# A graph network whose last three tiles, padding alone, are no longer gathered or scattered row by row

## Chip, cores and metric

The kernel runs on one core of a Trainium2 chip. The metric is the device time of one execution in microseconds (us); the median of three runs of the kernel before is 15976.06 us (15976.02, 15976.06 and 15996.48).

## What is computed

12500 nodes with 64 features and 212500 edges, sorted by destination, go through four graph layers. Each of them reads a row of a node table for every edge, computes a message from it and sums the messages by node. Cut to what matters here:

```python
# L0: softmax over the nodes gives attn; then
msg = h[src][:, None, :] * attn[src][:, :, None]
neigh = segment_sum(msg, dst, n)
# L1: two linear halves of [x[row], x[col]], relu, sum by row
# L2: three GAT layers
e = leaky_relu(alpha_src[src] + alpha_dst[dst], 0.2)
m = segment_max(e, dst, n)
ex = exp(e - m[dst])
out = segment_sum(alpha[:, :, None] * h[src], dst, n)
# L3: a three-layer network on [x[src], edge_attr], then sum by dst, then on the nodes
```

The output is the 12500 x 64 node table after L3.

## The kernel before

The edges are padded to 212992 = 1664 tiles of 128 edges. Sixteen tiles are a group (`GT = 16`), four groups a turn of the loops (`G4`, with four sets of buffers), and there are `TURNS = 26` turns. A padding edge has node 12500 at both ends, one row past the real ones. The real edges fill 1660 tiles and 20 rows of tile 1660, so tile 1660 holds 108 padding edges, and tiles 1661 to 1663, the last three of group k = 3 of the last turn, hold nothing else.

The program is a row of phases. A phase (`Phase.run`, line 91) gives each engine its own instruction stream, and ends with a barrier of all engines (lines 93 to 105). There the profile shows a DRAIN of each engine. Six phases run over all 1664 tiles with one indirect DMA per tile on GpSimd (POOL):

- `first_pass` (phase e0): gathers 64 floats per edge; TensorE multiplies them with the 0/1 matrix of equal destinations (`sums`, line 560) and counts edges per node (`counts`); GpSimd at 406 to 416, TensorE's loop at 579 to 585.
- `sort_rows` (phase sort1): computes for each edge a destination in the order of the other end, and scatters its row of 65 floats to `sorted_rows` (GpSimd at 1027 to 1041); the next phase (`carried_pass`) reads them.
- `gat_pass` three times (phases eg1, eg2, eg3): gathers 136, 136 and 65 floats per edge; VectorE starts a group when its 16 gathers have landed (line 1388, then the operation of line 1390).
- `attr_pass` (phase e3): gathers 128 floats per edge; TensorE starts a group's first quad of tiles when the 16 gathers have landed (`pe_first`, line 1622, operations of lines 1594 and 1595).

GpSimd's program is the same in the five gathering phases: a loop of 26 turns, in it the four groups, in each a wait for the row numbers (`loaded`), a wait per four tiles for the buffers (`summed`) and 16 calls of `gather` (line 112). Each gather adds 16 to the semaphore `gathered[k]`; the reader waits for all 16 gathers of a group at once. In the sorting phase the calls are of `scatter` (line 117), and GpSimd waits at the end for all that moved (line 1041). TensorE, VectorE and ScalarE have their last turn written out already in sort1, eg1 to eg3 and (TensorE and ScalarE) e3; GpSimd has all 26 turns in the loop everywhere, and TensorE has in e0. After a gathering phase, `finish_sums` reads what the phase stored.

Of the kernel before, what the change touches and what calls it, by code (L numbers as in the profile page):

```python
# [38 lines left out]
G4 = range(4)  # L39
B2 = range(2)  # L40
TURNS = NG // len(G4)
assert T % P == 0 and QT * DE == P and NT % CHUNK == 0 and N < P * P


# [83 lines left out]
def row_numbers(e, ve, c, out, pos, tmp):  # L128

    e.tensor_scalar(out, pos, 0x7FFFFFFF ^ (GROUP - 1), None, ALU.bitwise_and).then_inc(ve, 1)  # L130
    e.tensor_scalar(tmp, pos, P - 1, 4, ALU.bitwise_and, ALU.logical_shift_left).then_inc(ve, 1)
    e.wait_ge(ve, c(2))
    e.tensor_tensor(out, out, tmp, ALU.bitwise_or).then_inc(ve, 1)
    e.wait_ge(ve, c(1))
    e.tensor_scalar(tmp, pos, 7, GT - 1, ALU.logical_shift_right, ALU.bitwise_and).then_inc(ve, 1)
    e.wait_ge(ve, c(1))
    e.tensor_tensor(out, out, tmp, ALU.bitwise_or).then_inc(ve, 1)
    e.wait_ge(ve, c(1))


def broadcast_row(row, n):
# [27 lines left out]
class Kernel:  # L169
# [126 lines left out]
    def first_pass(self, table, out, last):  # L296
# [109 lines left out]
        def gpsimd(e):  # L406
            for k in G4:
                e.dma_start(ph.prime(), self.ident[0:16, 0:1]).then_inc(gathered[k].sem, 16)
            with e.Fori(0, TURNS) as it:
                for k in G4:  # L410
                    e.wait_ge(loaded[k].sem, loaded[k].at(it, 1))
                    for t in range(GT):
                        if t % QT == 0:
                            e.wait_ge(summed.sem, summed.at(it, (k + 1) * QUADS - U + t // QT))
                            e.sem_inc(turns, 1)
                        gather(e, got[k][:, t, :], table[:, :], rows[k][:, t, 1:2]).then_inc(gathered[k].sem, 16)

        def vector(e):
            e.sem_inc(equaled.sem, equaled.ahead)
# [124 lines left out]
        def tensor(e):  # L544
            e.sem_inc(summed.sem, summed.ahead)
            e.sem_inc(counted.sem, counted.ahead)
            e.wait_ge(set_up, 1)
            e.matmul(ps_count[:, :, :], zero[:, 0:P], zero[:, :], start=True, stop=False)

            def spread_keys(it, q):  # L550
                k, tiles = at(q)
                if q % QUADS == 0:
                    e.wait_ge(keyed.sem, keyed.at(it, k + 1))
                e.wait_ge(equaled.sem, equaled.at(it, q - 1))
                for i in range(QT):
                    t = tiles.start + i
                    last_i = e.transpose(ps_key[q % 2][:, i, :], key[k][:, t:t + 1].to_broadcast([P, P]), self.ident[:, :])  # L557
                last_i.then_inc(spread.sem, 1)

            def sums(it, q):  # L560
                k, tiles = at(q)
                e.wait_ge(gathered[k].sem, gathered[k].at(it, 1))
                e.wait_ge(equaled.sem, equaled.at(it, q + 1))
                e.wait_ge(copied.sem, copied.at(it, q - 1))
                for i in range(QT):
                    t = tiles.start + i
                    last_i = e.matmul(ps_sum[q % 2][:, i, 0:D], equal[k % 2][:, t, :], got[k][:, t, :], start=True, stop=True)  # L567
                last_i.then_inc(summed.sem, 1)

            def counts(it, q):  # L570
                e.wait_ge(hots.sem, hots.at(it, q + 1))
                e.wait_ge(hots_a.sem, hots_a.at(it, q + 1))
                for i in range(QT):
                    for end in B2:
                        last_i = e.matmul(ps_count[:, end, :], hot[q % 2][:, 0, end, i, :], hot[q % 2][:, 1, end, i, :],
                                          start=False, stop=False)
                last_i.then_inc(counted.sem, 1)

            with e.Fori(0, TURNS) as it:
                for q in range(U + 1):  # L580
                    if q < U:
                        spread_keys(it, q)
                    if q:
                        counts(it, q - 1)
                        sums(it, q - 1)
            e.matmul(ps_count[:, :, :], zero[:, 0:P], zero[:, :], start=False, stop=True).then_inc(opened, 1)
            e.wait_ge(scanned, 2)
            e.matmul(off_ps[:, :], self.above[:, :], incl[:, :, P - 1], start=True, stop=True).then_inc(offsets, 1)
# [197 lines left out]
    def sort_rows(self):  # L786
# [47 lines left out]
        numbers = Tally(ph, "numbers", 5 * n4)  # L834
        placed = Tally(ph, "placed", n4)
        moved = [Tally(ph, f"moved{k}", 1, GT * 16, ahead=16) for k in G4]
        first, table0, ready, turns = (ph.sem(k) for k in ("first", "table0", "ready", "turns"))

        def at(q):
            k, i = divmod(q, QUADS)  # L840
# [186 lines left out]
        def gpsimd(e):  # L1027
            for k in G4:
                e.dma_start(ph.prime(), self.ident[0:16, 0:1]).then_inc(moved[k].sem, 16)
            with e.Fori(0, TURNS) as it:  # L1030
                for k in G4:
                    e.wait_ge(placed.sem, placed.at(it, k + 1))
                    e.wait_ge(carried.sem, carried.at(it, (k + 1) * 2))
                    e.sem_inc(turns, 1)
                    for t in range(GT):
                        if t and t % QT == 0:
                            e.wait_ge(look_read.sem, look_read.at(it, (k + 1) * QUADS + t // QT - 2))
                            e.sem_inc(turns, 1)
                        scatter(e, self.sorted_rows, dest[k][:, t:t + 1], rows[k][:, t, :]).then_inc(moved[k].sem, 16)
            for k in G4:  # L1040
                e.wait_ge(moved[k].sem, moved[k].at(0, TURNS))
        ph.run(sync=sync, vector=vector, tensor=tensor, scalar=scalar, gpsimd=gpsimd)

    def carried_pass(self, values, out, last):
# [169 lines left out]
    def gat_pass(self, name, table, out, last, values, heads, ch):  # L1214
# [82 lines left out]
        def gpsimd(e):  # L1297
            for k in G4:
                e.dma_start(ph.prime(), self.ident[0:16, 0:1]).then_inc(gathered[k].sem, 16)
            with e.Fori(0, TURNS) as it:  # L1300
                for k in G4:
                    e.wait_ge(loaded[k].sem, loaded[k].at(it, 1))
                    for t in range(GT):
                        if t % QT == 0:
                            e.wait_ge(summed.sem, summed.at(it, (k + 1) * QUADS - U + t // QT))
                            e.sem_inc(turns, 1)
                        gather(e, got[k][:, t, :], table[:, :], rows[k][:, t, 1:2]).then_inc(gathered[k].sem, 16)

        def dve_key(e, it, k):
            e.wait_ge(loaded[buf(k)].sem, loaded[buf(k)].at(it, 1 + k // len(G4)))  # L1310
# [56 lines left out]
        def dve_stage(e, it, new, mid, old):  # L1367
# [17 lines left out]
                e.tensor_copy(c3[:, 2], r[:, 1]).then_inc(cuts.sem, 1)  # L1385
            if mid is not None:
                e.wait_ge(filled.sem, filled.at(it, mid + 1))
                e.wait_ge(gathered[buf(mid)].sem, gathered[buf(mid)].at(it, 1 + mid // n4))
                e.wait_ge(message.sem, message.at(it, mid))
                e.tensor_tensor(diff[:, :, :], by_tile(sm[:, 1, 0:W]), rows_mid[:, :, HF:FG], ALU.add).then_inc(scores.sem, 1)  # L1390
                e.wait_ge(scores.sem, scores.at(it, 4 * mid + 1))
                e.scalar_tensor_tensor(score[:, :, :], diff[:, :, :], 0.2, diff[:, :, :], ALU.mult, ALU.max).then_inc(scores.sem, 1)  # L1392
# [88 lines left out]
    def attr_pass(self, name, table, out, last, weights, own_weights):  # L1481
# [59 lines left out]
        def gpsimd(e):  # L1541
            for k in G4:
                e.dma_start(ph.prime(), self.ident[0:16, 0:1]).then_inc(gathered[k].sem, 16)
            with e.Fori(0, TURNS) as it:
                for k in G4:
                    e.wait_ge(loaded[k].sem, loaded[k].at(it, 1))
                    for t in range(GT):
                        if t % QT == 0:
                            e.wait_ge(summed.sem, summed.at(it, (k + 1) * QUADS - U + t // QT))
                            e.sem_inc(turns, 1)  # L1550
                        gather(e, got[k][:, t, :], table[:, :], rows[k][:, t, 1:2]).then_inc(gathered[k].sem, 16)

        def pe_own_turn(e, b):
            ts = own_quads[b]
# [32 lines left out]

        def pe_first(e, it, q):
            k, tiles = at(q)
            e.wait_ge(gathered[k % n4].sem, gathered[k % n4].at(it, 1 + k // n4))  # L1590
            e.wait_ge(attr_down.sem, attr_down.at(it, q + 1))
            e.wait_ge(relued.sem, relued.at(it, q - 1))
            for i in range(QT):
                e.transpose(ps_first[q % 2][:, i, :], got[k % n4][:, tiles.start + i, :], self.ident[:, :])  # L1594
                last_i = e.matmul(ps_first[q % 2][:, i, :], w_attr[:, i, :], attr_t[q % 4][:, :], start=False, stop=True,  # L1595
                                  skip_group_check=True)
            last_i.then_inc(first.sem, 1)
# [1481 lines left out]
```

## Time and profile before

| | |
|---|---|
| median of three runs | 15976.06 us |
| the profiled execution | 15981.7 us |
| its span, first to last instruction | 15980.0 us |
| granted TensorE clock, mean | 0.697 |
| POOL busy | 11257.5 us, 70% |
| PE (matmul) busy | 8190.7 us, 51% |
| VectorE (DVE) busy | 6692.7 us, 42% |
| ScalarE (ACT) busy | 5666.0 us, 35% |
| indirect DMAs of the six phases | 4992 + 3328 gathers, 1664 scatters |
| software DMA queue (GpSimd's) | 361120 packets, 582.27 MB, 15.9% of the 16 engines |

All rows are of one execution. A busy time of POOL in an indirect DMA is the time in which it makes the descriptors, not the time in which the data moves. A time after "idle before" is how long the engine had nothing to do before the instruction, and "<-" says what ended that. A wait that ended with a landing is read as: the instruction started when the DMA's data had arrived.

### The profile page before, as it was taken

How to read it: one execution, taken by the hardware profiler on the slowest of the kernel's cores; microseconds unless marked ns; L12 is line 12 of the kernel's file. 1: busy time of each engine (PE TensorE's matmuls, PEld its weight loads, DVE VectorE, ACT ScalarE, POOL GpSimd, SP SyncE). 2: the span in 40 equal slices, each digit the busy share in tenths (PEclk: the TensorE clock that was granted, in tenths of full speed). 3: DMA queues.
4: the chain of work that ended last, by engine and by line, in shares of the span. 5: the costliest groups of instructions: out<-in, count | busy, mean ns of one | idle time of the engine just before them, and what ended most of it. 6: DMA issues, size and time to landing. Idle time of an engine off the chain costs nothing. (4 is left out here: it accounts for less than half of the span.)

```text
span 15980.0 us, 259817 instructions
## 1 busy us (share of the span) xinstructions
PE 8190.7 (51%) x75456; PEld 7411.3 (46%) x75456; DVE 6692.7 (42%) x24144; ACT 5666.0 (35%) x13371; POOL 11257.5 (70%) x11862
## 2 busy tenths in 40 slices
PE   6555552565664763434432444432344444888886
PEld 4555441455554653333332333332344443777775
DVE  5555554777775863333335333335222224211112
ACT  2555551677774531222221222221111112333332
POOL 4777767677775457777767777776777775577776
PEclk9776765878877975666665666665555555799998
DMA  4444442222223743444432444443333332344443
GB/s 153 162 161 162 162 142 57 96 93 91 92 93 120 257 155 93 146 146 146 146 117 72 146 146 146 146 143 60 77 85 85 85 85 54 119 146 146 146 146 97
DMA packets 895395, 1965.03 MB, mean 123 GB/s; under 512 B 392230, under 2 KB 471026, under 8 KB 854067
## 3 DMA queue, kind: packets, MB, share of 16 engines
q0 software_dynamic: 361120, 582.27, 15.9%
q1 hardware_dynamic: 426179, 797.11, 14.6%
q10 hardware_dynamic: 107776, 582.40, 9.5%
q14 instruction: 243, 1.99, 0.0%
q8 instruction: 77, 1.26, 0.0%
HBM read 1095.74 MB, written 894.54 MB: 125 GB/s over the span
## 5 line engine op out<-in xcount | busy, mean ns | idle before, releaser
L112 POOL DMA_INDIRECT eg_got<-gat_table,eg_rows x4992 | 4714.7, 944 | 1542.1 <-issue 1512.5
L112 POOL DMA_INDIRECT e_got<-table,e_rows x3328 | 3155.6, 948 | 1031.2 <-issue 1004.6
L1321 PE MATMUL eg_ps_sum<-eg_got,eg_equal 128*128 128x136 f32 (+1 forms) x9984 | 2070.8, 382 | 280.3 <-DVE eg_got L1409 256.5
L1328 ACT ACTIVATE eg_outs<-eg_ps_sum 128x544 f32<-128x544 f32 (+1 forms) x1248 | 675.1, 541 | 4279.2 <-PE eg_ps_sum L1321 4268.9
L1321 PEld LDWEIGHTS eg_ps_sum<-eg_got,eg_equal 128*128 128x128 f32 x9984 | 1965.5, 291 | 344.2 <-ACT eg_outs L1328 189.1
L117 POOL DMA_INDIRECT sorted_rows<-sort_rows,sort_dest x1664 | 1615.9, 971 | 532.8 <-issue 495.9
L1353 PE MATMUL eg_small<-ident,eg_score 128*128 128x128 f32 (+1 forms) x312 | 138.6, 444 | 3176.1 <-DVE eg_score L1392 3176.1
L1353 PEld LDWEIGHTS eg_small<-ident,eg_score 128*128 128x128 f32 (+1 forms) x312 | 47.2, 151 | 3203.5 <-DVE eg_score L1392 3203.5
L1390 DVE TENSOR_TENSOR eg_diff<-eg_small,eg_got 128x128 f32<-128x128 f32 (+1 forms) x312 | 79.1, 253 | 2732.6 <-DMA eg_got<-gat_table,eg_rows 2732.6
L1621 DVE TENSOR_SCALAR e_got<-e_ps_second 128x512 f32<-128x512 f32 x416 | 287.6, 691 | 1758.0 <-PE e_ps_second L1604 1727.5
L567 PE MATMUL e_ps_sum<-e_got,e_equal 128*128 128x64 f32 x3328 | 628.8, 352 | 676.1 <-DMA e_got<-table,e_rows 676.1
L1421 ACT ACTIVATE eg_equal<-eg_equal_b 128x512 f32<-128x512 bf16 x1248 | 778.4, 624 | 469.1 <-issue 271.5
L567 PEld LDWEIGHTS e_ps_sum<-e_got,e_equal 128*128 128x128 f32 x3328 | 586.7, 265 | 694.6 <-DMA e_got<-table,e_rows 374.8
L449 DVE TENSOR_SCALAR e_hot<-iota_free,e_part_f 128x128 bf16<-128x128 bf16 x4992 | 880.2, 277 | 0.0
L897 DVE SCALAR_TENSOR_TENSOR sort_junk<-sort_ps_bc,sort_num,sort_before 128x128 bf16<-128x128 f32 (+3 forms) x1664 | 814.7, 545 | 48.2 <-PE sort_ps_bc L946 47.2
L496 ACT ACTIVATE e_dist<-iota_free,e_part_f 128x128 bf16<-128x128 bf16 x1664 | 528.2, 389 | 558.2 <-DVE e_part_f L437 378.9
L443 DVE TENSOR_TENSOR e_equal<-e_ps_key,e_key 128x512 f32<-128x512 f32 x416 | 286.4, 688 | 936.2 <-PE e_ps_key L557 932.9
L1594 PE MATMUL e_ps_first<-ident,e_got 128*128 128x128 f32 x1664 | 489.3, 294 | 368.0 <-DMA e_got<-table,e_rows 368.0
L1595 PE MATMUL e_ps_first<-e_attr_t,w_w_attr 128*128 128x128 f32 x3328 | 634.8, 293 | 0.0
L1206 POOL TENSOR_TENSOR e_cut<-e_rest,e_cut 128x256 bf16<-128x256 f32 x416 | 301.5, 725 | 460.8 <-ACT e_cut L1182 460.8
L1409 DVE TENSOR_TENSOR eg_got<-eg_got,eg_small 128x2048 f32<-128x2048 f32 (+1 forms) x312 | 602.7, 1932 | 10.6
L1595 PEld LDWEIGHTS e_ps_first<-e_attr_t,w_w_attr 128*128 128x128 f32 x3328 | 558.6, 210 | 0.0
(528 smaller groups left out, 20828.1 us busy)
## 6 DMA issues: line engine op xcount, KB each, us to landing
gat_out<-eg_outs ACTq DMA_DIRECT2D x208, 1152.0 KB
eg_equal_b<-equal_d SPq DMA_DIRECT2D x312, 512.0 KB
out<-e_outs ACTq DMA_DIRECT2D x208, 512.0 KB
out<-e_outs ACTq DMA_DIRECT2D x104, 1024.0 KB
values<-e_zeros_b SPq DMA_DIRECT2D x104, 768.0 KB
values_q<-e_zeros_b SPq DMA_DIRECT2D x104, 768.0 KB
sort_value<-values_q SPq DMA_DIRECT2D x104, 768.0 KB
e_value<-values SPq DMA_DIRECT2D x104, 768.0 KB
```

Of the source, the lines that this page charges most:

```text
L112: return e.indirect_dma_start(out, None, table, bass.IndirectOffsetOnAxis(ap=index, axis=0), **kw)
L117: return e.indirect_dma_start(table, bass.IndirectOffsetOnAxis(ap=index, axis=0), rows, None, **kw)
L449: last_i = e.tensor_scalar(hot[q % 2][:, a, end, i, :], self.iota_free[:, :], part_f[k % 2][:, a, end, t:t + 1], None, ALU.is_equal)
L496: e.activation(dist[q % 2][:, i, :], self.iota_free[:, :], ACT.Abs, scale=-1.0, bias=part_f[k % 2][:, 1, 1, t:t + 1]).then_inc(dist_made.s ...
L567: last_i = e.matmul(ps_sum[q % 2][:, i, 0:D], equal[k % 2][:, t, :], got[k][:, t, :], start=True, stop=True)
L897: last = e.scalar_tensor_tensor(junk[n - 1][:, 0:n, :], ps_bc[q % 2][:, 0:n, :], num[k % n4][:, 2, t:t + 1], before[:, QT - n:QT, :], ALU. ...
L1321: last_i = e.matmul(ps_sum[q % 2][:, i, 0:FG], equal[q % 4][:, i, :], got[k][:, t, :], start=True, stop=True)
L1328: e.activation(outs[k % 2][:, tiles, 0:FG], ps_sum[q % 2][:, :, 0:FG], ACT.Copy).then_inc(copied.sem, 1)
L1409: e.tensor_tensor(hs, hs, over(weight, ch), ALU.mult).then_inc(message.sem, 1)
L1421: e.activation(equal[q % 4][:, :, :], equal_b[buf(k)][:, tiles, :], ACT.Copy).then_inc(equaled.sem, 1)
L1594: e.transpose(ps_first[q % 2][:, i, :], got[k % n4][:, tiles.start + i, :], self.ident[:, :])
L1595: last_i = e.matmul(ps_first[q % 2][:, i, :], w_attr[:, i, :], attr_t[q % 4][:, :], start=False, stop=True, skip_group_check=True)
```

## The change

`REAL` counts the real tiles of each group of the last turn: [16, 16, 16, 13]. GpSimd's loop takes 25 turns, and the last one is written out with `REAL[k]` tiles. The readers of the last group wait for 13 gathers instead of 16 (`arrived`). In the sorting phase, the last three tiles, which stay where they are in the sorted order, are copied by one direct DMA of 128 partitions x 780 bytes, with a semaphore of its own. TensorE's loop in `first_pass` gets its last turn written out too, so that the wait can differ there. The arithmetic on the three tiles stays; it reads what an earlier group left in the buffer, and its results go to the padding node alone.

```diff
+REAL = [min(GT, max(0, -(-E // P) - ((TURNS - 1) * len(G4) + k) * GT)) for k in G4]
...
+def arrived(gathered, it, k):
+    buf, turn = k % len(G4), k // len(G4)
+    missing = GT - REAL[buf] if isinstance(it, int) and it + turn == TURNS - 1 else 0
+    return gathered[buf].at(it, 1 + turn) - 16 * missing
...
 # first_pass, gat_pass and attr_pass, GpSimd
-            with e.Fori(0, TURNS) as it:
+            def group(it, k, tiles):
+                e.wait_ge(loaded[k].sem, loaded[k].at(it, 1))
+                for t in range(tiles):
+                    if t % QT == 0:
+                        e.wait_ge(summed.sem, summed.at(it, (k + 1) * QUADS - U + t // QT))
+                        e.sem_inc(turns, 1)
+                    gather(e, got[k][:, t, :], table[:, :], rows[k][:, t, 1:2]).then_inc(gathered[k].sem, 16)
+            with e.Fori(0, TURNS - 1) as it:
                 for k in G4:
...
+                    group(it, k, GT)
+            for k in G4:
+                group(TURNS - 1, k, REAL[k])
 # first_pass, TensorE
-                e.wait_ge(gathered[k].sem, gathered[k].at(it, 1))
+                e.wait_ge(gathered[k].sem, arrived(gathered, it, k))
...
-            with e.Fori(0, TURNS) as it:
+            def turn(it):
                 for q in range(U + 1):
...
+            with e.Fori(0, TURNS - 1) as it:
+                turn(it)
+            turn(TURNS - 1)
 # sort_rows, GpSimd: group() as above with scatter; after the tiles of a group
+                if tiles < GT:
+                    e.dma_start(by_group(self.sorted_rows)[it * n4 + k, :, tiles:, :], rows[k][:, tiles:, :]).then_inc(tail_moved, 16)
...
+            for k in G4:
+                e.wait_ge(moved[k].sem, moved[k].at(0, TURNS) - 16 * (GT - REAL[k]))
+            e.wait_ge(tail_moved, 16 * sum(tiles < GT for tiles in REAL))
 # gat_pass, VectorE, and attr_pass, TensorE: the same arrived() in the wait for the gathers
```

## Rows read from the trace of the kernel before

**Rows 1.** Groups by line, engine POOL: count | busy us, mean ns | idle before.
```profile
L112 POOL DMA_INDIRECT eg_got<-gat_table,eg_rows x4992 | 4714.7, 944 | 1542.1 <-issue 1512.5 <-DMA eg_rows<-pairs_d 21.3 <-PE eg_ps_sum L1321 8.2
L117 POOL DMA_INDIRECT sorted_rows<-sort_rows,sort_dest x1664 | 1615.9, 971 | 532.8 <-issue 495.9 <-ACT sort_rows L1015 26.3 <-DVE sort_base L907 10.7
L112 POOL DMA_INDIRECT g1c_agg<-gat_out,end_row x98 | 125.5, 1281 | 36.9 <-issue 29.3 <-DVE g1c_agg L2822 7.6
```

**Rows 2.** Timeline of e0's end: start us, us busy, what [idle before].
```profile
2342.01 0.94 POOL L112 DMA_INDIRECT e_got<-table,e_rows  x1 [0.30 <-issue]
2344.55 1.97 PE L567 MATMUL e_ps_sum<-e_got,e_equal 128*128 128x64 f32 x8 [6.70 <-DMA e_got<-table,e_rows]
...
2362.07 0.94 POOL L112 DMA_INDIRECT e_got<-table,e_rows  x1 [0.30 <-issue]
2367.68 1.97 PE L567 MATMUL e_ps_sum<-e_got,e_equal 128*128 128x64 f32 x8 [9.60 <-DMA e_got<-table,e_rows]
```

**Rows 3.** Timelines, ends of eg1 and eg2.
```profile
8228.99 0.94 POOL L112 DMA_INDIRECT eg_got<-gat_table,eg_rows  x1 [0.30 <-issue]
8231.58 0.29 DVE L1390 TENSOR_TENSOR eg_diff<-eg_small,eg_got 128x128 f32<-128x128 f32 x1 [8.45 <-DMA eg_got<-gat_table,eg_rows]
8248.98 0.94 POOL L112 DMA_INDIRECT eg_got<-gat_table,eg_rows  x1 [0.30 <-issue]
8253.74 0.29 DVE L1390 TENSOR_TENSOR eg_diff<-eg_small,eg_got 128x128 f32<-128x128 f32 x1 [13.59 <-DMA eg_got<-gat_table,eg_rows]
...
10780.84 0.94 POOL L112 DMA_INDIRECT eg_got<-gat_table,eg_rows  x1 [0.30 <-issue]
10785.35 0.29 DVE L1390 TENSOR_TENSOR eg_diff<-eg_small,eg_got 128x128 f32<-128x128 f32 x1 [12.85 <-DMA eg_got<-gat_table,eg_rows]
```

**Rows 4.** DMA queues: GpSimd's queue in 2347:2357 and in 2363:2368: packets, MB, share.
```profile
q0 software_dynamic: 256, 0.26, 14.1%
...
q0 software_dynamic: 67, 0.07, 31.9%
```

**Rows 5.** Timeline of e3's end.
```profile
15753.65 0.94 POOL L112 DMA_INDIRECT e_got<-table,e_rows  x1 [0.30 <-issue]
15754.05 0.27 PE L1586 MATMUL e_ps_at<-ident,e_attrs 128*128 128x128 f32 x1
15758.79 0.48 PE L1594 MATMUL e_ps_first<-ident,e_got 128*128 128x128 f32 x1 [4.46 <-DMA e_got<-table,e_rows]
```

**Rows 6.** Windows of e3's end: length, busy (x count) by engine, PEclk, DMA share, GB/s.
```profile
15742.84:15754.30 11.46, 11.46 (x93) 10.20 (x91) 2.07 (x3) 5.69 (x13) 8.72 (x10) 1.00 0.28 51
15758.79:15763.90 5.11, 5.11 (x31) 4.66 (x32) 0.69 (x1) 1.12 (x2) 0.00 (x0) 0.73 0.36 149
```

**Rows 7.** Timeline of sort1's end.
```profile
5020.47 0.97 POOL L117 DMA_INDIRECT sorted_rows<-sort_rows,sort_dest  x1 [0.30 <-issue]
...
5023.01 0.96 POOL L117 DMA_INDIRECT sorted_rows<-sort_rows,sort_dest  x1 [0.30 <-issue]
5032.99 0.35 SPq L1103 DMA_DIRECT2D e_group_f<-sorted_rows  x1
```

**Rows 8.** POOL's sequencer at sort1's end, line 93: durations ns, first and last start.
```profile
L93 POOLq DRAIN  x1: 6603/6603/6603, 5025.5 to 5025.5; - x1
```

**Rows 9.** The first direct DMAs of GpSimd in eg3, and SP's wait for the first.
```profile
11217.50 2.06 POOL L1299 DMA_DIRECT2D eg_prime<-ident  x4 [4.41 <-POOLq L105]
11223.92 0.35 SPq L1293 DMA_DIRECT2D eg_rows<-pairs_d  x1
```

**Rows 10.** POOL's sequencer, the branch of e0's loop (line 409), all turns.
```profile
L409 POOLq COMPARE_BRANCH  x26: 40/45/53, 342.3 to 2348.0; - x26
```

**Rows 11.** Timeline: written-out gathers beside a VectorE scan.
```profile
2406.86 3.62 DVE L1837 TENSOR_TENSOR_SCAN f_run<-links,f_acc_t 64x1664 f32<-64x1664 bf16 x1 [7.43 <-ACT f_acc_t L1813]
2407.49 3.74 POOL L112 DMA_INDIRECT f_pr_spans<-span,first_key  x1 [0.30 <-issue]
2411.53 0.94 POOL L112 DMA_INDIRECT f_pr_spans<-span,first_key  x1 [0.30 <-issue]
```

More of the change, by code:

```diff
@@ L408, in gpsimd @@
                 e.dma_start(ph.prime(), self.ident[0:16, 0:1]).then_inc(gathered[k].sem, 16)
-            with e.Fori(0, TURNS) as it:
-                for k in G4:
[L411 to L416, printed above, removed]
+            def group(it, k, tiles):
[6 more added lines that the diff above has]
+            with e.Fori(0, TURNS - 1) as it:
+                for k in G4:
+                    group(it, k, GT)
+            for k in G4:
+                group(TURNS - 1, k, REAL[k])
         def vector(e):
@@ L836, in sort_rows @@
         moved = [Tally(ph, f"moved{k}", 1, GT * 16, ahead=16) for k in G4]
-        first, table0, ready, turns = (ph.sem(k) for k in ("first", "table0", "ready", "turns"))
+        first, table0, ready, turns, tail_moved = (ph.sem(k) for k in ("first", "table0", "ready", "turns", "tail_moved"))
         def at(q):
@@ L1029, in gpsimd, with group @@
                 e.dma_start(ph.prime(), self.ident[0:16, 0:1]).then_inc(moved[k].sem, 16)
-            with e.Fori(0, TURNS) as it:
-                for k in G4:
[L1032 to L1039, printed above, removed]
+            def group(it, k, tiles):
+                e.wait_ge(placed.sem, placed.at(it, k + 1))
+                e.wait_ge(carried.sem, carried.at(it, (k + 1) * 2))
+                e.sem_inc(turns, 1)
+                for t in range(tiles):
+                    if t and t % QT == 0:
+                        e.wait_ge(look_read.sem, look_read.at(it, (k + 1) * QUADS + t // QT - 2))
+                        e.sem_inc(turns, 1)
+                    scatter(e, self.sorted_rows, dest[k][:, t:t + 1], rows[k][:, t, :]).then_inc(moved[k].sem, 16)
+                if tiles < GT:
+                    e.dma_start(by_group(self.sorted_rows)[it * n4 + k, :, tiles:, :], rows[k][:, tiles:, :]).then_inc(tail_moved, 16)
+            with e.Fori(0, TURNS - 1) as it:
+                for k in G4:
+                    group(it, k, GT)
             for k in G4:
-                e.wait_ge(moved[k].sem, moved[k].at(0, TURNS))
+                group(TURNS - 1, k, REAL[k])
+            for k in G4:
+                e.wait_ge(moved[k].sem, moved[k].at(0, TURNS) - 16 * (GT - REAL[k]))
+            e.wait_ge(tail_moved, 16 * sum(tiles < GT for tiles in REAL))
         ph.run(sync=sync, vector=vector, tensor=tensor, scalar=scalar, gpsimd=gpsimd)
@@ L1299, in gpsimd, with group @@
                 e.dma_start(ph.prime(), self.ident[0:16, 0:1]).then_inc(gathered[k].sem, 16)
-            with e.Fori(0, TURNS) as it:
-                for k in G4:
[L1302 to L1307, printed above, removed]
+            def group(it, k, tiles):
+                e.wait_ge(loaded[k].sem, loaded[k].at(it, 1))
+                for t in range(tiles):
+                    if t % QT == 0:
+                        e.wait_ge(summed.sem, summed.at(it, (k + 1) * QUADS - U + t // QT))
+                        e.sem_inc(turns, 1)
+                    gather(e, got[k][:, t, :], table[:, :], rows[k][:, t, 1:2]).then_inc(gathered[k].sem, 16)
+            with e.Fori(0, TURNS - 1) as it:
+                for k in G4:
+                    group(it, k, GT)
+            for k in G4:
+                group(TURNS - 1, k, REAL[k])
         def dve_key(e, it, k):
@@ L1387, in dve_stage @@
                 e.wait_ge(filled.sem, filled.at(it, mid + 1))
-                e.wait_ge(gathered[buf(mid)].sem, gathered[buf(mid)].at(it, 1 + mid // n4))
+                e.wait_ge(gathered[buf(mid)].sem, arrived(gathered, it, mid))
                 e.wait_ge(message.sem, message.at(it, mid))
@@ L1543, in gpsimd, with group @@
                 e.dma_start(ph.prime(), self.ident[0:16, 0:1]).then_inc(gathered[k].sem, 16)
-            with e.Fori(0, TURNS) as it:
-                for k in G4:
[L1546 to L1551, printed above, removed]
+            def group(it, k, tiles):
+                e.wait_ge(loaded[k].sem, loaded[k].at(it, 1))
+                for t in range(tiles):
+                    if t % QT == 0:
+                        e.wait_ge(summed.sem, summed.at(it, (k + 1) * QUADS - U + t // QT))
+                        e.sem_inc(turns, 1)
+                    gather(e, got[k][:, t, :], table[:, :], rows[k][:, t, 1:2]).then_inc(gathered[k].sem, 16)
+            with e.Fori(0, TURNS - 1) as it:
+                for k in G4:
+                    group(it, k, GT)
+            for k in G4:
+                group(TURNS - 1, k, REAL[k])
         def pe_own_turn(e, b):
@@ L1589, in pe_first @@
             k, tiles = at(q)
-            e.wait_ge(gathered[k % n4].sem, gathered[k % n4].at(it, 1 + k // n4))
+            e.wait_ge(gathered[k % n4].sem, arrived(gathered, it, k))
             e.wait_ge(attr_down.sem, attr_down.at(it, q + 1))
```

## The prediction

> **What bounds the kernel now.** I read the groups by line first. In the six phases that run over all 1664 tiles, POOL makes an indirect DMA's descriptors for 944 to 971 ns, then sits for some 300 ns, and nearly all of that idle time is "issue": it waits for nobody [rows 1]. From the eg row, (4714.7 + 1542.1) / 4992 = 1.253 us per gather on average; at the ends of the phases a step is 0.94 + 0.30 = 1.25 us [rows 2, 3]. From the sort row (1615.9 + 532.8) / 1664 = 1.29 us, at its end 1.27 [rows 7]. So the phases go at POOL's pace, and what matters is what their last group hangs on.
>
> Next I read the timelines of the ends. In e0, TensorE has been idle 9.60 us when the last group's gathers have landed [rows 2]. In eg1 and eg2 VectorE has been idle about 13 us, and eg3 is built the same way [rows 3]. In e3 TensorE has been idle 4.46 us [rows 5]. In the sorting phase the last scatter starts at 5023.01; once GpSimd's wait for the landings is over, its DRAIN of 6.6 us begins, at 5025.5, and the next phase starts at 5032.99 [rows 7, 8]. In all six ends the last indirect DMA is on the path, and everything behind it is a chain that moves with it.
>
> A second thing is to be seen there. A group's data are ready 1.60 us after its last gather was issued in an ordinary group (2342.95 to 2344.55), but 4.67 us after it in the last group (2363.01 to 2367.68) [rows 2]. In eg1 it is 1.65 against 3.82 us [rows 3]. Packets on GpSimd's queue explain it: 14.1% of 16 engines x 10 us over 256 packets is 88 ns each in ordinary tiles, and 31.9% of 16 x 5 us over 67 is 381 ns each at e0's end [rows 4]. The last four tiles are those whose edges (108, 128, 128 and 128 of 128) all read the same row of the table. I call the 4.67 - 1.60 us, and its like in the other phases, the excess.
>
> **The change, part by part.**
> *Issue time.* In each of e0, eg1, eg2 and eg3 three gathers go: 3 x 1.25 = 3.75 us, four times is 15.0 us. All of it is on the path, since the engine that waits has been idle for longer.
> *The excess.* e0: 4.67 - 1.60 = 3.07. eg1: 3.82 - 1.65 = 2.17. eg2: 10781.78 to 10785.35 is 3.57, less 1.65: 1.92 [rows 3]. eg3 repeats the pattern, and I count it like eg2. Sum 9.1. Tile 1660 with its 108 equal rows stays last, so not all of it goes. Bounds: nothing of it goes, or all. The excess builds up over four nearly equal gathers and three of them go, so I take three quarters: 6.8 us.
> *e3.* Here the idle time caps the gain. TensorE is done with the group before at 15754.3 (its last matmul, 15754.05 + 0.27), and the landing moves from 15758.79 to about 15754.59 - 3.75 + 2.5 = 15753.3, so TensorE's 4.46 us idle time vanishes, and no more [rows 5]. But after that idle time the clock stood at a mean of 0.73 in the first quad, which took 5.1 us (15758.79 to 15763.90); without a stall three quads take 11.46 us, 3.8 each, at a clock of 1.00 [rows 6]. That is up to 1.3 us more, of which I take 1.0, since the clock need not be up from the first matmul on. Sum 5.5 us; from below 3.75 (the landing's tail stays as long, no clock), from above 6.
> *The sorting phase.* Three scatters go; the direct copy takes the place of the first (5020.47). It waits for nothing of its own and has 13 scatters ahead of it in GpSimd's queue. The trace has no copy of this shape. From a scatter's start to the DRAIN, with its landing between them, it is 2.5 us (5023.01 to 5025.5) [rows 7, 8]. The direct DMAs at the start of eg3 take 2.06 / 4 = 0.5 us each of GpSimd, and SP, which waits for the first, goes on 6.4 us after its start (11217.50 to 11223.92) [rows 9]. So the DRAIN would begin between 5021.0, if the copy landed with its own issue, and 5026.9: a gain of 4.5 to a loss of 1.4. I take the scatter's time, being the nearest in partitions and place: 5023.0, a gain of 2.5 us. The DRAIN behind it I leave at 6.6 us; that its length changes by a microsecond with what lies in the queue can't be excluded. The added wait on `tail_moved` has nothing behind it but that DRAIN.
> *The written-out turns.* GpSimd's sequencer took the loop's last branch at 2348.0, while the last gather began at 2362.07 [rows 2, 10]: it runs 14 us, some eleven gathers, ahead of the engine. Leaving the loop one turn earlier and reading code that is used once is hidden behind these. TensorE's written-out turn in e0 is hidden behind its waits for gathers (6.70 us before group k = 2 of the last turn, with its 16 ordinary gathers) [rows 2]; without that cover each microsecond of it counts. I cost both at nothing. What is late next, once the stalls are shorter, is TensorE itself in e3; in e0 and eg1 to eg3 it is still the landing.
>
> Sum: 15.0 + 6.8 + 5.5 + 2.5 = 29.8 us. Against the profiled execution that is 15981.7 - 29.8 = 15951.9; the median of the runs lies 5.6 us lower, which gives 15946 us.
>
> **The rivals.**
> *Only the issue time goes* (nothing of the excess). Tile 1660 is nearly all padding, and if one such gather is enough to keep the packets slow, the landing's tail stays. For it: the packets that land last are the slowest. Against it: gathers overlap, and at 88 ns per packet before them the slowness is theirs alone [rows 4]. Gain 15.0 + 3.75 + 2.5 = 21.3: 15955 us. A page would have it so: the Trainium skill, "DMA: Bandwidth & Descriptors", section on the anatomy of one DMA on the GpSimd path, gives each such DMA a fixed 2.0 us plus its bytes over the bandwidth, whatever rows it reads; a gather of eg1 (69632 bytes) would be there 2.2 us after its start, in the last tile as in any. The trace disagrees: 8248.98 to 8253.74 is 4.76 us [rows 3].
> *All of the excess goes*, with e3 at its best: 15.0 + 9.1 + 6 + 2.5 = 32.6: 15943.5 us.
> *Written-out gathers are slow: slower than before.* Place: the written-out turn on GpSimd, 61 DMAs in six phases. The straight-line gathers of g1c cost (125.5 + 36.9) / 98 = 1.66 us each, 0.40 more than in the loops [rows 1]. At that price 6 x 61 x 0.40 = 148 us are added, 118 net: 16094 us. It turns the sign from 0.08 us per gather on. Against it: another straight line of gathers takes 0.94 us each, as the loops do, except one of 3.74 us that lies over a VectorE scan of 3.62 [rows 11]. So the slowness comes from what VectorE does beside them, not from the code. The Trainium skill, "SBUF — State Buffer", section on the two sides of SBUF, says that a VectorE operation that holds the port pair shared with GpSimd keeps it from writing descriptors; by that rule, and by the trace, straight code costs nothing of itself.
> *The change does nothing that can be measured*: something else, such as the stores, ends the phases. The idle times of rows 2 and 3 speak against it. 15976 us.
>
> **How the numbers follow.** A difference of 0.2%, 32 us, is about what a measurement of this kernel tells from none; 15944 is that bound. Chances: my forecast (26 to 31 us less) 0.56, all of the excess 0.22, only the issue time 0.15, slower 0.03, nothing 0.04. Single runs of one kernel lie up to 20 us apart, so I give each case some 6 us to both sides: of the forecast 0.21 falls beyond the bound, of the second case 0.16, of the third 0.01. Together faster 0.38, the same 0.58, slower 0.04. Range: the largest gain, 15.0 + 9.1 + 6 + 4.5 = 35, gives 15941, with the measurement 15936. The smallest sum of the bounds, 15.0 + 0 + 3.75 - 1.4 - 1 = 16, gives 15960, with the measurement 15966.
>
> **What would show it.** Right: 4983 and 3322 gathers at an unchanged 0.94 us; in e0 to eg3 the wait's end 5.2 to 6.0 us earlier counted from the phase's first gather, 2.0 to 2.4 us behind the last gather's end; in e3 no idle TensorE before its last group, and a clock of 1.00 there; a copy that lands 2 to 3 us after its start and a DRAIN of about 6.6 us. Wrong: idle time above 0.30 us between GpSimd's DMAs in the last turn, TensorE short of code in e0's last turn, a copy that holds the wait past 5025, or a tail behind the last gather that stays at 3.6 us and more.

## The result and the profile after

The changed kernel's median is 15951.62 us (15945.77 to 15954.14, 22 runs), that of the kernel before on the same chip 15979.92 us (15976.02 to 15996.48, 22 runs). The ratio is 0.9982, with a 95% interval of 0.9975 to 0.9988: 28.3 us less by the medians. The profiled executions say 15953.09 against 15981.7 us, 28.6 us less. Forecast were 15946 us and a gain of 29.8.

The groups of POOL after the change, by line (they answer to [rows 1]); columns as there:

```profile
L113 POOL DMA_INDIRECT eg_got<-gat_table,eg_rows x4983 | 4705.4, 944 | 1538.8 <-issue 1511.5 <-DMA eg_rows<-pairs_d 20.8 <-PE eg_ps_sum L1350 6.4
L113 POOL DMA_INDIRECT e_got<-table,e_rows x3322 | 3149.4, 948 | 1030.9 <-issue 1002.2 <-DMA e_rows<-pairs_d 16.0 <-PE e_ps_sum L1649 11.8
L118 POOL DMA_INDIRECT sorted_rows<-sort_rows,sort_dest x1661 | 1612.7, 971 | 532.0 <-issue 492.2 <-ACT sort_rows L1031 26.1 <-DVE sort_base L923 13.4
```

Three operations fewer per phase, each as long as before, and the idle time is still "issue". Now the ends, after the change, as a timeline; first e0 (against [rows 2]):

```profile
2342.20 0.95 POOL L113 DMA_INDIRECT e_got<-table,e_rows  x1 [0.30 <-issue]
...
2357.31 0.95 POOL L113 DMA_INDIRECT e_got<-table,e_rows  x1 [0.30 <-issue]
2360.65 1.97 PE L580 MATMUL e_ps_sum<-e_got,e_equal 128*128 128x64 f32 x8 [4.13 <-DMA e_got<-table,e_rows]
```

The last group has 13 gathers, and its data are ready 2.39 us behind the last one's end (2358.26 to 2360.65); before it was 4.67. TensorE still waits for them, 4.13 us instead of 9.60. In eg1, eg2 and eg3 (against [rows 3]) VectorE starts 2.4 to 2.5 us behind the last gather's end:

```profile
8237.92 0.29 DVE L1419 TENSOR_TENSOR eg_diff<-eg_small,eg_got 128x128 f32<-128x128 f32 x1 [6.78 <-DMA eg_got<-gat_table,eg_rows]
...
10765.20 0.29 DVE L1419 TENSOR_TENSOR eg_diff<-eg_small,eg_got 128x128 f32<-128x128 f32 x1 [7.41 <-DMA eg_got<-gat_table,eg_rows]
...
13285.47 0.18 DVE L1419 TENSOR_TENSOR eg_diff<-eg_small,eg_got 128x16 f32<-128x16 f32 x1 [7.99 <-DMA eg_got<-gat_table,eg_rows]
```

In e3 (against [rows 5]) the wait before the last group is gone. The first row below is the last matmul of group k = 2, the second and third are the last group's, without idle time before them:

```profile
15731.21 1.06 PE L1649 MATMUL e_ps_sum<-e_got,e_equal 128*128 128x128 f32 x8
15732.10 0.27 PE L1620 MATMUL e_ps_at<-ident,e_attrs 128*128 128x128 f32 x1
15732.21 0.27 PE L1628 MATMUL e_ps_first<-ident,e_got 128*128 128x128 f32 x1
```

And the windows of the same stretch (against [rows 6]): the last group's first 11.46 us are done at the full clock, as the group before it.

```profile
15720.64:15732.10 11.46, 11.46 (x94) 10.42 (x93) 2.32 (x4) 5.64 (x12) 5.78 (x7) 1.00 0.18 42
...
15732.10:15743.56 11.46, 11.46 (x95) 10.42 (x94) 2.08 (x3) 5.62 (x12) 0.00 (x0) 1.00 0.23 94
```

The sorting phase's end, timeline and POOL's sequencer (against [rows 7, 8]):

```profile
5012.69 0.96 POOL L118 DMA_INDIRECT sorted_rows<-sort_rows,sort_dest  x1 [0.30 <-issue]
5013.65 0.61 POOL L1056 DMA_DIRECT2D sorted_rows<-sort_rows  x1
5023.22 0.35 SPq L1127 DMA_DIRECT2D e_group_f<-sorted_rows  x1
```

```profile
L94 POOLq DRAIN  x1: 6440/6440/6440, 5015.9 to 5015.9; - x1
```

**Where the time went.** Whole phases are poor measures here: earlier stalls make one and the same phase up to 2 us longer or shorter between executions (e0 of the changed kernel took 2115.4 us in one execution and 2117.3 in another). What is comparable is the end of a phase: from the start of the last group's first gather or scatter to the clearing of the phase's semaphores (in e0 after the change 2342.20 to 2392.16). I use it for all kernels:

| us | e0 | sort1 | eg1 | eg2 | eg3 | e3 | sum |
|---|---|---|---|---|---|---|---|
| before | 55.47 | 28.52 | 41.97 | 42.32 | 40.88 | 52.19 | 261.35 |
| after | 49.96 | 25.26 | 37.55 | 36.89 | 36.01 | 46.90 | 232.57 |
| less | 5.51 | 3.26 | 4.42 | 5.43 | 4.87 | 5.29 | 28.78 |
| forecast | 6.0 | 2.5 | 5.4 | 5.2 | 5.2 | 5.5 | 29.8 |

The forecast row is the prediction's, its 6.8 us of excess shared out by its own shares. The six ends hold the whole gain of 28.6 us. Between them single stretches differ, but the differences cancel: from the clearing behind eg2 to eg3's first gather it is 425.9 us after the change and 422.1 before, and the other stretches are together as much shorter.

### The profile page after: what moved, and what is told of

The parts are those of the page before. It is cut to its first block and busy times, and to the rows that moved or that the text cites. A ratio compares the mean times of both kernels' runs of the same rounds, so it can differ in the third digit from the quotient of the medians.

```text
span 15951.4 us, 259671 instructions
## 1 busy us (share of the span) xinstructions
PE 8184.6 (51%) x75456; PEld 7411.5 (46%) x75456; DVE 6693.9 (42%) x24144; ACT 5665.9 (36%) x13371; POOL 11240.2 (70%) x11845
## 5 line engine op out<-in xcount | busy, mean ns | idle before, releaser
L970 PE MATMUL sort_ps_table<-sort_hot_lo,sort_hot_hi 128*128 128x128 bf16 x1664 | 187.9, 244 | 728.0 <-ACT sort_table L1022 727.2
```

## The experiments

Each was timed beside the kernel before on the same chip. Single executions of one kernel differ by 5 to 20 us, so a difference of 3 or 4 us is read from the ends of the phases, and the medians are given beside it. "Landing" is from the end of the last gather to the last of its data.

**Written-out turns, nothing left out.**

```diff
-REAL = [min(GT, max(0, -(-E // P) - ((TURNS - 1) * len(G4) + k) * GT)) for k in G4]
+REAL = [GT] * 4
...
-            e.wait_ge(tail_moved, 16 * sum(tiles < GT for tiles in REAL))
```

> The changed kernel with all 1664 tiles gathered and scattered again: GpSimd's last turn of each of the six phases and TensorE's last turn of e0 are still written out, nothing is left out. Theory (written-out code costs nothing, the gain is all in the missing gathers): within 5 us of the kernel before, 15975 to 15985 by a profile; gathers of the last turn at the same median pitch of 1.25 us as in the loop; landing behind the last gather 3.5 to 4.6 us as before. Rival (the written-out instructions are issued slower than looped ones): last turns longer, anywhere up to 118 us above the kernel before. A second rival: the loop's end costs something that the written-out turn shares, so that part of the 28 us gain comes from here: 5 to 15 us faster than before.

Measured: 15974.02 us against 15975.21, ratio 0.9999 (0.9990 to 1.0008). The ends sum to 260.65 us against 261.35. The last turn's gathers go on at the same pace. All gathers of the last 100 us of e0, in this kernel:

```profile
L113 POOL DMA_INDIRECT e_got<-table,e_rows x80: 940/944/992, 2263.9 to 2363.0; - x80
its engine sat idle before it (us, times) until:
  issue: 24.4, 80
```

0.944 us each and 24.4 / 80 = 0.305 us between two. The medians differ by 1.2 us, but their interval reaches some 14 us to each side, so they would not rule out the second rival; the ends do, being 0.7 us shorter in sum. To within that, the written-out code costs nothing and brings nothing; both rivals fall, and the gain is in what was left out.

**The same gathers, other rows.** The kernel before, with only the data of the padding edges changed:

```diff
+    spread = (N + np.arange(EP - E) % (NP - N)).astype(np.int32)
...
-        line = np.concatenate([a.pop(k), pad])
+        line = np.concatenate([a.pop(k), spread if k == "src" else pad])
```

> The kernel before, all 1664 tiles gathered, with one change in the data that the host lays out: the padding edges' source goes round the 44 padding nodes of the node table in place of naming one row. Theory (gathers of one same row 128 times land late): the landing behind the last gather falls from 3.5 to 4.6 us to about 1.6 us in e0, eg1, eg2 and eg3, 9.1 us in all, and e3 gives up to 2.6 us, so 9 to 12 us faster than the kernel before. Rival (the last gathers land late because they are the last, whatever they read: the completion of a queue that runs empty): the landing stays at 3.5 to 4.6 us, the time within 3 us of the kernel before.

Measured: 15960.75 us against 15975.21, ratio 0.9991 (0.9982 to 1.0000): 14.5 us less by the medians. The landing fell from 4.61, 3.75, 3.48 and 3.54 us to 1.43, 1.50, 1.50 and 1.38, and the ends of e0, eg1, eg2 and eg3 became 3.20, 1.93, 2.28 and 2.18 us shorter: 9.6 us together, where the excess had been put at 9.1. (With e3 the ends give 9.9 of the 14.5 us; the rest of the difference of the medians lies outside the ends and is not explained.) The end of e0 in this kernel (against [rows 2]):

```profile
2361.67 0.94 POOL L112 DMA_INDIRECT e_got<-table,e_rows  x1 [0.30 <-issue]
2364.08 1.97 PE L567 MATMUL e_ps_sum<-e_got,e_equal 128*128 128x64 f32 x8 [6.60 <-DMA e_got<-table,e_rows]
```

GpSimd's queue in 2359:2364, while the last gathers are issued, and in 2363:2368, of this kernel (against [rows 4]):

```profile
q0 software_dynamic: 141, 0.13, 10.2%
...
q0 software_dynamic: 32, 0.03, 2.5%
```

That is 10.2% of 16 engines x 5 us over 141 packets, 58 ns each, and 62 ns in the second; the equal rows took 381 [rows 4]. These means are mixed ones: about half of the queue's packets in each window have 4 bytes and took 9 ns. The packets with data (2048 bytes in e0), counted by themselves in the same traces, took 168 ns each in the ordinary tiles and 787 with equal rows in the kernel before, and 115 and 117 here. Same instructions, same place, same bytes: that the last gathers landed late was due to their 128 equal rows, not to their being the last. The Trainium skill ("DMA: Bandwidth & Descriptors", anatomy of one DMA on the GpSimd path) puts a DMA at 2.0 us plus its bytes over the bandwidth; an estimate by it for a gather of 32768 bytes is 2.0 us + 0.08, whatever it reads. With spread rows e0's last gather lands 0.94 + 1.43 = 2.37 us behind its start, near that; with equal rows it is 0.94 + 4.61 = 5.55, and the measurement decides.

The forecast of this run for e3, up to 2.6 us, missed: its end is 0.35 us shorter. The timeline of this kernel shows two reasons (ACTq is ScalarE's queue):

```profile
15717.49 0.33 PE L1594 MATMUL e_ps_first<-ident,e_got 128*128 128x128 f32 x1 [1.40 <-DMA e_got<-table,e_rows]
...
15733.21 0.36 ACTq L1647 DMA_DIRECT2D out<-e_outs  x1
...
15734.94 0.94 POOL L112 DMA_INDIRECT e_got<-table,e_rows  x1 [0.30 <-issue]
15738.71 0.47 PE L1594 MATMUL e_ps_first<-ident,e_got 128*128 128x128 f32 x1 [6.06 <-DMA e_got<-table,e_rows]
```

TensorE had waited only 1.40 us for group k = 2 (6.15 in the kernel before), was done with it earlier, and its 1 MB of sums was stored from 15733.21 on, over the last gathers. Their landing took 2.79 us; in the next kernel, where no store lies over them, it took 1.46. (Why TensorE was ahead is not shown. The edges of group k = 2 are the same in both kernels.) The second reason is the clock. TensorE had now been idle for 6.06 us in place of 4.46, and the granted clock of its next 5.11 us was 0.51, against 0.73 in [rows 6]:

```profile
15738.71:15743.82 5.11, 5.11 (x22) 4.45 (x23) 0.00 (x0) 1.11 (x2) 0.00 (x0) 0.51 0.01 3
```

So TensorE starts the last group 1.36 us earlier, counted from the group's first gather (22.50 against 23.86 us), and needs 1.0 us more from there to the phase's end (29.33 against 28.33).

**The rest of the excess.** The changed kernel, with the padding edges of tile 1660 spread over the 44 padding nodes, in ascending order:

```diff
+    spread = (N + np.minimum(np.arange(EP - E) * (NP - N) // 108, NP - N - 1)).astype(np.int32)
...
-        line = np.concatenate([a.pop(k), pad])
+        line = np.concatenate([a.pop(k), spread if k == "src" else pad])
```

> The changed kernel, with the 108 padding edges of the last gathered tile spread in ascending order over the 44 padding nodes. Theory (rows that repeat are what is left of the late landing): 2.4 us behind the last gather become about 1.6 us in four phases, 3.2 us in all, and 0 to 0.8 us in e3; 3 to 4 us faster than the changed kernel. Rival (2.4 us is what any last gather takes to land): landing stays at 2.3 to 2.4 us, no difference.

Measured: 15943.62 us against 15975.21, ratio 0.9980 (0.9971 to 0.9989), 31.6 us less. Landing 1.44, 1.53, 1.51 and 1.43 us in place of 2.35, 2.41, 2.39 and 2.34. The ends of these phases: 48.55, 35.89, 35.63 and 35.03 us, 5.3 less than after the change, and e3 0.4 less. (The landings account for 3.6 of the 5.3; the rest lies behind them and is not explained.) So some 60% of the excess went with the three tiles (2.26 + 1.34 + 1.09 + 1.20 = 5.9 us of landing), the other 3.6 us of landing were tile 1660's.

**The sorting phase as before.** The changed kernel, but all 16 tiles of the last group are scattered by row:

```diff
-                group(TURNS - 1, k, REAL[k])
+                group(TURNS - 1, k, GT)
...
-                e.wait_ge(moved[k].sem, moved[k].at(0, TURNS) - 16 * (GT - REAL[k]))
-            e.wait_ge(tail_moved, 16 * sum(tiles < GT for tiles in REAL))
+                e.wait_ge(moved[k].sem, moved[k].at(0, TURNS))
```

> The changed kernel with the sorting phase scattering all 16 tiles of its last group by row, as before; the gathers stay at 13. Theory (the scatters of the last three tiles and what they wait for were worth 3.6 us by the two profiles, 2.5 by the forecast): 2.5 to 3.6 us slower than the changed kernel, the last scatter of the sorting phase 2 to 4 us later, POOL's last DRAIN of the phase with it. Rival (that difference is chance between two executions): within 1 us of the changed kernel.

Measured: 15951.07 us against 15975.21, ratio 0.9985 (0.9976 to 0.9994): 24.1 us less, some 4 less than the changed kernel brings. The sorting phase's end is 28.52 us, exactly that of before. The last scatter starts at 5018.09 and the DRAIN, as in [rows 8] 6603 ns long, at 5020.6:

```profile
L94 POOLq DRAIN  x1: 6603/6603/6603, 5020.6 to 5020.6; - x1
```

The sorting phase is worth 3.26 us. In e3 of this execution TensorE waited 1.79 us for the last group's landing, and the end is 45.36 us, the shortest of all.

**The changed kernel again.**

> The changed kernel once more, as the measure for the two kernels beside it. Theory (its phases repeat within a microsecond; the stretch between eg2 and eg3 of 425.9 us, against 422.1 before, was chance): 26 to 31 us faster than the kernel before, that stretch 420 to 422 us. Rival (the change lengthens that stretch by 4 us): 425 to 426 us again.

Measured: 15968.41 us against 15996.28, ratio 0.9983 (0.9974 to 0.9992), 27.9 us less. In this set of runs both kernels had medians 16 to 21 us above those of the others, so the kernels in it are compared with each other alone. The ends sum to 232.27 us (232.57 in the first profile), and the stretch between eg2 and eg3 was 422.0 us: the change does not lengthen it, and the 425.9 was one execution's.

**How far the gain goes.**

```diff
+SORTED = REAL
+REAL = [GT, GT, GT, 8]
...
-                group(TURNS - 1, k, REAL[k])
+                group(TURNS - 1, k, SORTED[k])
```

> Leaves out part of the computation: the last group's gathers are cut to 8 tiles in all five gathering phases, so five tiles of real edges are worked with old data; the sorting phase is that of the changed kernel. Theory (a gather that goes is worth its 1.25 us only until the engine that waits for the landing has no idle time left: 4.1 us of TensorE in e0, 6.5 to 6.8 of TensorE and VectorE in eg1 to eg3, none in e3): e0 4 to 5 us shorter, eg1, eg2, eg3 6.3 to 6.8 us each, e3 0 to 0.5 us; 23 to 26 us faster than the changed kernel. Rival (every phase goes at the gathers' pace to its end, the excess included): 5 x 1.25 + 0.9 = 7.15 us in each of five phases, 35.7 us faster.

Measured: 15947.46 us against 15968.41 for the changed kernel: 21.0 us less (ratio to before 0.9969, 0.9957 to 0.9982). That is far from the 35.7 of an uncapped gain, but also less than the 23 to 26 expected. Against the first profile of the changed kernel the ends became shorter by 4.1 us in e0, 5.1, 4.1 and 6.8 in eg1, eg2 and eg3 and not at all in e3 (46.95 us). e0, eg3 and e3 are as expected. In eg1 and eg2 the gain is smaller than the 6.3 to 6.8 expected, and the timeline of this kernel's eg1 points to a third limit:

```profile
8236.93 0.36 ACTq L1364 DMA_DIRECT2D gat_out<-eg_outs  x1
...
8242.37 0.29 DVE L1421 TENSOR_TENSOR eg_diff<-eg_small,eg_got 128x128 f32<-128x128 f32 x1 [2.92 <-DMA eg_got<-gat_table,eg_rows]
```

The last gather is issued from 8236.81 to 8237.76, so the landing took 4.5 us (in eg2 4.9), though its rows are ordinary. Beside it runs the store of the group before, 1152 KB; the queues in 8238:8242:

```profile
q10 hardware_dynamic: 132, 1.05, 69.1%
q0 software_dynamic: 32, 0.07, 4.4%
```

The gather's packets were not slow but late: those with data took 168 ns each, but the last of them began 3.7 us behind the gather's end, in the run with spread rows 1.0 us. In eg3 the rows are half as long (65 floats against 136) and so is the store; it lies over the last gathers too, and the landing was 1.8 us. That the store is the cause is read from these timelines; no run moved the store alone.

**A version meant to beat both.** Only the 20 real rows of tile 1660 are gathered, and SyncE issues the direct copy:

```diff
 # GpSimd, the three gathering functions
+                    n = E % P if tiles < GT and t == tiles - 1 else P
-                    gather(e, got[k][:, t, :], table[:, :], rows[k][:, t, 1:2]).then_inc(gathered[k].sem, 16)
+                    gather(e, got[k][0:n, t, :], table[:, :], rows[k][0:n, t, 1:2]).then_inc(gathered[k].sem, 16)
 # sort_rows, SyncE, behind its loop; the copy is gone from GpSimd's group()
+            for k in G4:
+                if REAL[k] < GT:
+                    e.wait_ge(placed.sem, placed.at(TURNS - 1, k + 1))
+                    e.wait_ge(carried.sem, carried.at(TURNS - 1, (k + 1) * 2))
+                    e.dma_start(by_group(self.sorted_rows)[(TURNS - 1) * n4 + k, :, REAL[k]:, :], rows[k][:, REAL[k]:, :]).then_inc(tail_moved, 16)
```

> Meant to beat both kernels. In the five gathering phases the last gather fetches only the 20 rows of real edges of its tile (its 108 padding rows keep old data, which reaches padding nodes alone); in the sorting phase the direct copy of the last three tiles is issued by SyncE instead of by GpSimd behind its 13 scatters. Theory (equal rows are what is left of the late landing, and GpSimd's time is per descriptor): landing behind the last gather 2.3 to 2.4 falls to 1.5 us or below, the gather of 20 rows takes 0.2 to 0.6 us in place of 0.94; together 1.2 to 1.6 us in each of e0 and eg1 to eg3, 0 to 1.5 in e3; in the sorting phase the DRAIN begins 1.53 us behind the last scatter's end, as before the change, in place of 2.26: 0.7 us. Sum 6 to 9 us faster than the changed kernel, 34 to 37 us faster than the kernel before. Rival (a gather's time is fixed, however few rows): 0.94 us stays, sum 4 to 5 us. Second rival (the copy on SyncE's queue collides with the scatters or holds the phase's end): sorting phase not shorter than the changed kernel's 2127.6 us.

Measured: 15963.32 us against 15968.41 for the changed kernel and 15996.28 for the one before, ratio to before 0.9979 (0.9970 to 0.9988): 33.0 us less than before, 5.1 less than the change. The end of eg1, this kernel, with the gather of 20 rows last:

```profile
8239.51 0.95 POOL L113 DMA_INDIRECT eg_got<-gat_table,eg_rows  x1 [0.30 <-issue]
8240.76 0.91 POOL L113 DMA_INDIRECT eg_got<-gat_table,eg_rows  x1 [0.30 <-issue]
8243.28 0.29 DVE L1424 TENSOR_TENSOR eg_diff<-eg_small,eg_got 128x128 f32<-128x128 f32 x1 [6.52 <-DMA eg_got<-gat_table,eg_rows]
```

20 rows take 0.90 to 0.91 us of GpSimd (0.94 in e0), 128 take 0.94 to 0.95: the rival was right, the issue time is all but fixed. The landing fell to 1.33 to 1.54 us as the theory had it. The copy on SyncE collides with nothing: the DRAIN begins at 5022.8 behind a last scatter of 5020.23, and the sorting phase's end is 24.58 us, 0.73 shorter than in the run beside it (25.31). Its whole length, 2131.0 us against the 2127.6 of the second rival, says nothing on that: this execution's scatters came 1.276 us apart in place of 1.274, which is over 3 us in 1661. The ends sum to 225.86 us, 6.4 less than the changed kernel's 232.27: just inside the theory's 6 to 9, although its term for the issue time failed, and above the rival's 4 to 5. By the medians it is 5.1, between the two. This version and the one with spread rows (0.9980) can't be told apart by these runs; both lie below the changed kernel by the ends of all gathering phases.

## Why the prediction was right

*Issue time, 15.0 us.* Right. The operations kept their 0.94 us and the gaps their 0.30, and each of the four phases still waits for its last landing. The run with 8 tiles shows how long that lasts: TensorE's wait in e0 had 4.13 us left, and leaving out five gathers more (6.3 us) brought 4.1.

*The excess, 6.8 of 9.1 us.* The mechanism was right and is shown by the run that changed the rows alone: 9.6 us. The 88 and 381 ns per packet with which the prediction argued are halved by the 4-byte packets among them; for the packets with data it is 168 against 787 ns, and the argument stands. The share was somewhat too high: the landings became 5.9 us shorter, 62% of the whole and not three quarters, and the four ends 20.23 us, which leaves 5.2 for it (the 0.7 between lies behind the landings). The prediction took the excess to build up evenly over four tiles. A tile of 108 equal rows kept 0.9 us of it in each phase, 3.6 of 9.5, so the last tile holds more than its quarter. To that extent the rival that one such gather keeps the tail had a point.

*e3, 5.5 us.* Measured 5.29. TensorE's idle time of 4.46 us vanished and the clock stayed at 1.00. From the group's first gather to its first matmul on gathered rows it is 19.90 us in place of 23.86, 4.0 less where 4.46 was forecast, and from there to the end 27.01 in place of 28.33, 1.3 less where the clock was given 1.0. Executions of the same code differ here: with the other rows of tile 1660 or another sorting phase e3's end was 46.50 and 45.36 us, so 5.5 is good to about 1.5 us only. That TensorE is what bounds e3 now is shown by the run with 8 tiles (46.95 us with five gathers fewer). It does so narrowly: in the execution of 45.36 us it still waited 1.79 us for the landing.

*The sorting phase, 2.5 us.* Measured 3.26. The copy starts 0.30 us earlier than a fourteenth scatter would have, since no gap lies before it; the DRAIN begins 2.26 us behind its start in place of 2.5; and it is 0.16 us shorter. An estimate by the same section of the Trainium skill ("DMA: Bandwidth & Descriptors", anatomy of one DMA on the GpSimd path) is 2.0 us + 0.23 for this copy's 99840 bytes. The trace agrees with 2.26 us.

*The written-out turns, nothing.* Right, by the run in which nothing else was changed. The rival of slow written-out gathers (16094 us) is ruled out by it. That g1c's gathers are slow for what VectorE does beside them, as the prediction argued, can be counted in the trace of the kernel before: the 36 of them that overlap a VectorE operation of 2.0 us took 1.74 us in the mean, the other 62 took 1.02. Two neighbours, one of each kind:

```profile
8363.76 1.00 POOL L112 DMA_INDIRECT g1c_agg<-gat_out,end_row  x1 [0.30 <-issue]
...
8365.78 2.03 DVE L2732 TENSOR_TENSOR g1c_agg<-g1c_agg,g1c_mg_a 128x1792 f32<-128x1792 f32 x1 [0.55 <-ACT g1c_mg_b L2749]
8366.41 2.27 POOL L112 DMA_INDIRECT g1c_agg<-gat_out,end_row  x1 [0.30 <-issue]
```

*The sum.* Forecast 29.8, measured 28.8 in the six ends: 1.6 us less of the excess, 0.2 less in e3, 0.8 more in the sorting phase. The median came out higher than forecast by 5.6 us, of which 1.5 are the smaller gain. The other 4 are the reference's: the kernel before had 15979.92 us in the 22 runs beside the changed one, and 15976.06 in the three on which the forecast stood. The prediction held a difference below 32 us to be one that a measurement hardly tells from none; with 22 runs of each kernel the interval, 0.9975 to 0.9988, does tell 28.3 us from none. The rival "only the issue time" (21.3 us) is refuted by the shorter landings; "all of the excess" (32.6) describes not this kernel but the two made after it, which gained 31.6 and 33.0.

## What to carry to other kernels

Before you cut transfers from a pipeline, look at what each of its ends waits for: a gather removed was worth its full 1.25 us where an engine had been idle longer than that, and five more brought nothing in e3, where TensorE's 4.46 us of waiting were used up. Padding is not free because it is small: 128 indices that all name one row made the last gathers of every phase land 2 to 3 us late, and spreading them over the padding rows, with no instruction changed, brought a third of what leaving them out did by the ends of the phases (9.9 of 28.8 us), half by the medians (14.5 of 28.3). The wait of the engine behind them is not the only cap on such a gain: the last gathers can meet the store of the group before, and where they did, in two kernels here, they landed 1.3 to 3.4 us later. That is read from timelines and was not tried by itself.

## What the runs showed of the hardware

- GpSimd's time for an indirect DMA hardly follows its number of rows: 0.90 to 0.94 us for 20, 0.94 to 0.95 for 128.
- Packets of 2048 bytes that read one row again and again took 787 ns each, those of other rows 115 to 168 ns in the windows above (381 against 58 to 88 ns with the 4-byte packets of the same queue counted in). Whether the table's memory or something on the way is what they queue for was not tried.
- GpSimd's DRAIN at the end of the sorting phase is 6603 ns with 16 scatters in the last group, 6440 with 13 scatters and the direct copy, and 6358 with 13 scatters and the copy on another engine. At these three points that is 82 ns less for each DMA of GpSimd that this group has fewer; other numbers were not tried. I had left it at 6.6 us.
- TensorE's granted clock over the first 5.11 us of e3's last group was 0.73 after 4.46 us without work and 0.51 after 6.06 us; over the first 11.46 us it was 1.00 after 1.79 us without work, and 1.00 after none.
